# Reordered projections, halved softplus and paced clears in a Perceiver block with a selective scan

## The reference, cut to what matters

```
x = x + attention(layernorm(x), ctx)              # q, k, v of width 512, reshaped to (-1, 16, 64)
n = layernorm(x)
xi = n @ x_proj.T                                 # 1024 channels
xc = silu(causal_conv4(xi) + conv_b)
delta = softplus(n @ dt_proj.T + dt_b)
B, C = n @ B_proj.T, n @ C_proj.T                 # 16 states
h[s] = exp(delta * A[s]) * h[s] + delta * B[s] * xc    # along the 64 tokens, for each state s
y = sum over s of h[s] * C[s] + D * xc
x = x + y @ out_proj.T
x = x + experts(layernorm(x))                     # 16 experts, 4 per token, chosen by routed scores
```

## Time and profile before

| | us |
|---|---|
| three runs, median | 1340.01 |
| lowest, highest | 1334.44, 1340.54 |
| the profiled execution | 1334.18 |
| its span (first to last instruction) | 1332.2 |
| clearing: first issue of a clear | 84.94 |
| first projections of groups 0, 1, 2, 3 start on PE | 124.3, 353.1, 576.0, 798.7 |
| first block of the experts on PE | 898.98 |
| last slots of group 2 (dispatch begins) | 875.12 |

### The profile page before, as it was taken

The page is one execution under the profiler, slowest core; times in us unless marked ns, Lnnn a source line. Parts: engine busy times, 40 slices in busy tenths (PEclk is TensorE's granted clock), DMA queues, the critical chain, the costliest instruction groups (busy, mean ns, idle before and its releaser), DMA issues.

```text
span 1332.2 us, 13289 instructions
## 1 busy us (share of the span) xinstructions
PE 1143.1 (86%) x4276; PEld 729.0 (55%) x4276; DVE 881.5 (66%) x946; ACT 621.5 (47%) x1366; POOL 134.0 (10%) x113
## 2 busy tenths in 40 slices
PE   6988769789797899998889989629999999999992
PEld 4875646566564567675557757324444445444451
DVE  1311579666757999967799995877999974224312
ACT  4542665435355655537556635624455422222321
POOL 0010003201000043000007000030000000233002
PEclk9998889989998999999899999759999998999997
DMA  8375006998601145340035331068999984999994
GB/s 281 111 245 194 4 17 221 404 396 326 223 9 16 33 125 175 78 145 0 17 72 150 119 123 44 0 225 274 360 357 351 375 316 152 375 357 406 410 382 126
DMA packets 115188, 266.27 MB, mean 200 GB/s; under 512 B 11280, under 2 KB 44208, under 8 KB 115120
## 3 DMA queue, kind: packets, MB, share of 16 engines
q1 hardware_dynamic: 99248, 207.22, 45.1%
q0 software_dynamic: 15872, 58.20, 11.1%
HBM read 197.07 MB, written 68.32 MB: 199 GB/s over the span
## 4 chain that ended last, share of the span: by engine, by line
PE 46%; DVE 35%; DMA 8%; ACT 7%; issue 3%; POOL 1%; SPq 0%; POOLq 0%; DVEq 0%; ACTq 0%
DVE state L1348 12%; PE bank L815 9%; PE bank L776 7%; DVE state L1345 6%; PE bank L683 5%; PE bank L695 4%; PE bank L836 4%; PE bank L716 4%; DVE decay L1352 3%; DMA ctx<-in_ctx_t 3%; DVE state L1355 3%; DVE y_acc L1359 2%; PE bank L632 2%; DMA bc_bcast<-bc_scratch 2%; PE bank L747 2%
## 5 line engine op out<-in xcount | busy, mean ns | idle before, releaser
L1348 DVE TENSOR_TENSOR_SCAN state<-decay,state 128x2048 f32<-128x2048 f32 x64 | 282.9, 4421 | 23.5 <-ACT decay L1102 22.6
L815 PE MATMUL bank<-expert_w,block_x_t 128*128 128x512 f32 x496 | 227.0, 601 | 1.8 <-ACT block_x_t L1154 1.7
L683 PE MATMUL bank<-decay,params 128*128 128x512 f32 x384 | 173.3, 595 | 5.9 <-DVE decay L1352 5.9
L1639 POOL DMA_INDIRECT dispatched<-ffn_x,slot x32 | 73.0, 2280 | 756.3 <-DVE slot L1441 747.7
L1102 ACT ACTIVATE decay<-delta_even,params 128x256 f32<-128x256 f32 x256 | 107.2, 498 | 82.7 <-PE bank L683 74.2
L815 PEld LDWEIGHTS bank<-expert_w,block_x_t 128*128 128x128 f32 x496 | 91.6, 195 | 93.7 <-issue 91.6
L695 PE MATMUL bank<-ctx,queries_ctx 128*128 128x256 f32 x512 | 125.6, 403 | 16.2 <-DMA ctx<-in_ctx_t 15.0
L716 PE MATMUL bank<-probs,ctx 128*128 128x256 f32 x512 | 121.2, 392 | 11.1 <-ACT probs L1009 6.4
L1102 ACT ACTIVATE decay<-delta_odd,params 128x256 f32<-128x256 f32 x256 | 106.2, 499 | 34.5 <-PE bank L683 24.9
L695 PEld LDWEIGHTS bank<-ctx,queries_ctx 128*128 128x128 f32 x512 | 102.1, 204 | 34.2 <-DMA ctx<-in_ctx_t 16.4
L1496 DVE SCALAR_TENSOR_TENSOR hidden<-hidden,bank 128x256 f32<-128x256 f32 x62 | 26.1, 421 | 142.7 <-ACT hidden L1158 141.7
(11 more groups left out here) (193 smaller groups left out, 1334.2 us busy)
## 6 DMA issues: line engine op xcount, KB each, us to landing
dispatched<-ffn_x POOLq DMA_DIRECT2D x38, 1024.0 KB, 27.2
expert_w<-in_eg_t SPq DMA_DIRECT2D x62, 512.0 KB, 6.4
expert_w<-in_eu_t SPq DMA_DIRECT2D x62, 512.0 KB, 9.6
expert_w<-in_ed_t SPq DMA_DIRECT2D x62, 512.0 KB, 9.6
ctx<-in_ctx_t SPq DMA_DIRECT2D x32, 512.0 KB, 7.5
ctx<-in_ctx_n SPq DMA_DIRECT2D x32, 512.0 KB, 4.1
bc_bcast<-bc_scratch SPq DMA_DIRECT2D x64, 256.0 KB, 5.8
block_x<-dispatched SPq DMA_DIRECT2D x62, 256.0 KB, 9.0
```

Of the source, the lines that this page charges most:

```text
L683: mm = pe.matmul(y_bank[c][:, :], ident, dA[(g * NS + j) % NDEC][:, c * 512:(c + 1) * 512], start=False, stop=(j == NS - 1))
L815: mm = pe.matmul(o, xbT[q % 2][:, c, :], w_gu[q % NW][:, :, c, :], start=(c == 0), stop=(c == DC - 1))
L1348: dve.tensor_tensor_scan(h, dA[n % NDEC][:, 0:sw], h, 0.0, ALU.mult, ALU.add).then_inc(scan_rd, 1)
L1639: pool.indirect_dma_start(xd[WAVE_OF[c]], bass.IndirectOffsetOnAxis(slot[:, i:i + 1].bitcast(U32), 0), fx[:, t, :], None).then_inc(dispatc ...
```

## The change

It does six things. (1) The xp weights are loaded and multiplied before the dt weights, in SP's, PE's and ACT's lists; the scratch of softplus and tanh moves into the place of the xp weights. (2) The sums of states 14 and 15 come after all eight jobs, and `copy_sum` after the logarithm (for group 3's boundary: before it). (3) Softplus runs in two halves, the first after the second dt job, the tanh after the third; `scan_inputs` takes the tanh product first and then each half. (4) DVE puts the three parts of state 15 between the four convolutions, where before all of it stood ahead of them. (5) State 0 of group 3 is finished before the tokens of group 2 are normed, and `y_start(3)` goes ahead of that group's `norm_std`; the expert weights of blocks 1 and 2 are loaded after the first three token blocks. (6) The clears start at the same point as before, but each waits until the one before it has landed.

```
 CLEARS = [(w, r, min(r + CLEAR_ROWS, ROWS[w])) for w in range(len(WAVES)) for r in range(0, ROWS[w], CLEAR_ROWS)]
-CLEAR_UNITS = range(8, 16)
+CLEAR_FROM = 8
 JMAX = max(CAP) // P
...
 LEAD, TAIL, PRE = 4, 2, 2
-LN_AFTER = 3
 SCAN_PARTS = 4
...
                 out += [("probs", UNIT0[g] + k)]
-        out += [("v", g)] * DC + [("norm2", g)] * NTS[g] + [("bc", g)] + [("dt", g)] * (NBK // 2) + [("xp", g)] * (NBK // 2)
+        out += [("v", g)] * DC + [("norm2", g)] * NTS[g] + [("bc", g)] + [("xp", g)] * (NBK // 2) + [("dt", g)] * (NBK // 2)
         if g + 1 < NGR:
...
             xp = QT_[:, 4096:8192].rearrange("p (c n) -> p c n", c=DC)
-            sp_tmp = [QT_[:, 0:NBK * GTS[g]] for g in range(NGR)]
-            th_tmp = [QT_[:, SW:SW + NBK * GTS[g]] for g in range(NGR)]
+            sp_tmp = [QT_[:, 2 * SW:2 * SW + NBK * GTS[g]] for g in range(NGR)]
+            th_tmp = [QT_[:, 3 * SW:3 * SW + NBK * GTS[g]] for g in range(NGR)]
         del_s = [(del_0, del_1)[g % 2][:, 0:NBK * GTS[g]] for g in range(NGR)]
...
                 sp.wait_ge(x1_rdy, g + 1)
+                sp.dma_start(xp, xp_t.rearrange("(c p) n -> p c n", p=P)).then_inc(xpw_in, 16)
                 sp.dma_start(dtw, dt_t.rearrange("(c p) n -> p c n", p=P)).then_inc(dtw_in, 16)
-                sp.dma_start(xp, xp_t.rearrange("(c p) n -> p c n", p=P)).then_inc(xpw_in, 16)
             def bc_of(g):
...
                 if w == 0:
-                    for j in range(NW):
+                    load_gate_up(w, 0)
+                    load_down(w, 0)
+                    for j in range(NX):
+                        load_block_x(w, j)
+                    for j in range(1, NW):
                         load_gate_up(w, j)
                         load_down(w, j)
-                    for j in range(NX):
-                        load_block_x(w, j)
                     load_bc((NGR - 1) * NS + 3)
...
                 mm.then_inc(a_full, 1)
-                for w, landed in ((dtw, dtw_in), (xp, xpw_in)):
+                for w, landed in ((xp, xpw_in), (dtw, dtw_in)):
                     pe.wait_ge(landed, 16 * (g + 1))
...
                         mm.then_inc(a_full, 1)
-                        if g > 0 and w is dtw and k == NBK - 2:
-                            sum_state(g - 1, NS - 2)
-                        if g > 0 and w is xp and k == 2:
-                            sum_state(g - 1, NS - 1)
+
+                if g > 0:
+                    for s in range(NS - PRE, NS):
+                        sum_state(g - 1, s)
             def out_proj(g):
...
                 ins.then_inc(a_free, 1)
-            def softplus_exp(g):
-                act.wait_ge(a_free, CONV_JOBS[g])
-
-                step(act.activation(sp_tmp[g], del_s[g], ACT.Abs))
-                act.activation(sp_tmp[g], sp_tmp[g], ACT.Exp, scale=-1.0).then_inc(act_step, 1)
+            def halves(v, g, half):
+
+                n = NBK * GTS[g] // 2
+                return v[g][:, half * n:(half + 1) * n]
+
+            def softplus_exp(g, half):
+
+                act.wait_ge(a_free, ja.n)
+                v = halves(sp_tmp, g, half)
+                step(act.activation(v, halves(del_s, g, half), ACT.Abs))
+                act.activation(v, v, ACT.Exp, scale=-1.0).then_inc(act_step, 1)
                 chain.n += 1
...
                 act.wait_ge(act_step, chain.n)
-                act.activation(sp_tmp[g], sp_tmp[g], ACT.Ln, bias=1.0).then_inc(sp_rdy, 1)
+                for half in range(2):
+                    v = halves(sp_tmp, g, half)
+                    act.activation(v, v, ACT.Ln, bias=1.0).then_inc(sp_rdy, 1)
             def silu(g):
...
                 for k in range(0, NBK, 2):
-                    proj_dt(g, k)
+                    proj_x(g, k)
                     if late:
...
                 for k in range(0, NBK, 2):
-                    proj_x(g, k)
-                    if k == 0:
-                        softplus_exp(g)
-                    if k == 2 * (LN_AFTER - 1):
-                        softplus_ln(g)
-                    if g > 0 and k == 2:
-                        copy_sum(g - 1)
-                silu(g)
+                    proj_dt(g, k)
+                    if k == 4:
+                        silu(g)
+                    if k % 4 == 2:
+                        softplus_exp(g, k // 4)
+                if g == NGR - 1:
+                    copy_sum(g - 1)
+                softplus_ln(g)
+                if 0 < g < NGR - 1:
+                    copy_sum(g - 1)
                 if g + 1 < NGR:
...
             scan_decay(NGR - 1, 0)
+            y_start(NGR - 1)
             norm_std(NTS[NGR - 2])
             ffn_copy(NGR - 2)
-            y_start(NGR - 1)
             ffn_logits(NGR - 2)
...
                 d = del_s[g]
-                dve.wait_ge(sp_rdy, g + 1)
-                step(dve.scalar_tensor_tensor(out=d, in0=d, scalar=0.0, in1=sp_tmp[g], op0=ALU.max, op1=ALU.add))
                 dve.wait_ge(tanh_rdy, g + 1)
-
                 step(dve.scalar_tensor_tensor(out=th_tmp[g], in0=th_tmp[g], scalar=1.0, in1=u_s[g],
                                               op0=ALU.add, op1=ALU.mult))
-                step(dve.scalar_tensor_tensor(out=u_s[g], in0=th_tmp[g], scalar=0.5, in1=d,
-                                              op0=ALU.mult, op1=ALU.mult))
+                n = NBK * GTS[g] // 2
+                for half in range(2):
+                    h = slice(half * n, (half + 1) * n)
+                    dve.wait_ge(sp_rdy, 2 * g + half + 1)
+                    step(dve.scalar_tensor_tensor(out=d[:, h], in0=d[:, h], scalar=0.0, in1=sp_tmp[g][:, h],
+                                                  op0=ALU.max, op1=ALU.add))
+                    ins = dve.scalar_tensor_tensor(out=u_s[g][:, h], in0=th_tmp[g][:, h], scalar=0.5, in1=d[:, h],
+                                                   op0=ALU.mult, op1=ALU.mult)
+                step(ins)
                 first = d.rearrange("p (m t) -> p m t", t=T)[:, :, 0:1]
...
                     norm_apply(TILE0[g + 2], NTS[g + 2], NT, mv1_, rstd1, TILE0[g + 2])
-                for s in range(PRE):
+                for s in range(PRE - 1):
                     scan_step(g, late.pop(0))
                 for k in range(0, NBK, 2):
+                    if k // 2 in range(SCAN_PARTS - 1):
+                        scan_step(g, late[0], parts=(k // 2,))
                     conv(g + 1, k)
                 scan_inputs(g + 1)
-                if g + 1 < NGR - 1:
-                    scan_step(g + 1, 0, parts=(0, 1, 2))
+                scan_step(g + 1, 0)
                 add_tiles(g)
                 ffn_norm(g)
-                if g + 1 < NGR - 1:
-                    scan_step(g + 1, 0, parts=(3,))
-            scan_step(NGR - 1, 0, parts=(0, 1))
             route(NGR - 2)
-            scan_step(NGR - 1, 0, parts=(2, 3))
             slots(NGR - 2)
...
             pool.wait_ge(zero_rdy, 1)
+            pool.wait_ge(s_full, CLEAR_FROM)
             for i, (w, first, end) in enumerate(CLEARS):
-                n = CLEAR_UNITS[i * len(CLEAR_UNITS) // len(CLEARS)]
-                pool.wait_ge(s_full, n)
+                if i:
+                    pool.wait_ge(cleared, 16 * i)
                 v = xd[w][first:end].rearrange("(p r) d -> p r d", p=P)
...
```

## The result

The changed kernel took 1290.4 us (median of 4 runs, 1288.5 to 1291.31), the kernel before 1340.28 beside it (1334.44 to 1341.49): a ratio of 0.966, 95% interval 0.9618 to 0.9702. The forecast was 1295, its range 1281 to 1316. The profiled span fell from 1332.2 to 1289.4, by 42.8 us; the sum forecast 41.1.

| point | before | after | gained so far | by this stage | forecast |
|---|---|---|---|---|---|
| first projection, group 0 | 124.31 | 119.34 | 5.0 | 5.0 | 4.5 |
| first decay, group 0 | 165.83 | 159.73 | 6.1 | 1.1 | 3.5 |
| issue of the weights, group 1 | 342.17 | 309.43 | 32.7 | 26.6 | 25.8 |
| first projection, group 1 | 353.13 | 323.73 | 29.4 | -3.3 | 0.7 |
| first projection, group 2 | 576.02 | 538.44 | 37.6 | 8.2 | 5.3 |

A forecast was written before the change was run, and what follows sets the result against it. Bound: a chain of unlike stages, group 1's attention on transfers beside clears, group boundaries on a chain over all engines. Terms 5 - 0.5 + 26.5 + 3.5 + 10.6 - 2.5 - 1.5 = 41.1 us gave 1293.1, forecast 1295, range 1281 to 1316.

The forecast's parts named there:

- Attention 0: Up to group 0's first projection: last `ctx_n` lands sooner with one clear in flight, 5 us, less 0.5 for xp weights.
- What bounds attention 1: Group 1's attention waits on transfers slowed by queued clears, not arithmetic; pacing wins 25.8 us up to the weights' issue.
- The weights of group 1: From issue of group 1's projection weights to its first projection: they land sooner with paced clears, 0.7 us gained.
- Group 0: From group 0's first projection to its first decay, with no sums or state between: 3.5 us gained (0 to 6).
- Boundaries 1 and 2: At the boundaries of groups 1 and 2 queries resume 5.3 us earlier each, set by `out_proj` and no longer DVE.
- The last boundary: Group 3's first projection to group 2's last slots: state 0 now precedes the routing, slots about 6 us later.
- The handover: From the slots to the first expert block: last dispatch lands within 4 us instead of 7.43, 3.5 us gained.
- the weights: Expert weights of blocks 1 and 2, now after the first token blocks: 1.5 us lost (0 to -7.5).
- The end: The last stretch, from group 3's `out_proj` to the kernel's end: no gain forecast, 0 us.
- Clears still slow attention 1: Rival: one clear in flight is almost always moving, `ctx_t` stays late, half of 26.5 us lost: 1308 us; 17%.
- clears late: Rival: 40 landings in a row end late and hold DVE at `ffn_norm(0)`; at 9 us a clear, 1363 us; 5%.
- boundaries give nothing: Rival: convolutions hold ACT, ACT holds PE, late sums hold `out_proj`; 10.6 us and half of 3.5 lost: 1307; 13%.

The follow-up runs named there:

- the first run: The kernel before with only the paced clears, each clear waiting for the one before it: 1302.36 us, 0.9786 of the kernel before.
- the second run: The changed kernel without the paced clears, back in bursts of five at units 8 to 15: 1324.07 us, 0.9944 of the kernel before.

## Why the prediction was right, point by point

- **Attention 0** (4.5, measured 5.0): right. PE waited 0.74 us for the last probabilities in place of 4.62 for a `ctx_n`, and the 16 matmuls behind it took 3.72 us in place of 5.27.
- **What bounds attention 1** (25.8, measured 26.6): right, both sides were run. The paced clears alone took 28.6 us off the way to group 1's weights, and without them all of it was gone. DVE waited 2.7 us for broadcasts, in the kernel before 31.3. The pace was mis-sized, though: the forecast took DVE's 10.17 us a state, 50.8 for five, and 3 us of loss to transfers over eight units; from 214.78 to 267.92 five states took 53.1 us. The excess is two waits of 1.19 us for a broadcast, but PE ran 10.78 us a unit without a pause meanwhile, so they did not set the time. What was left of the loss in attention 1 was PE's work, not a transfer. That the gain comes of the pacing, and not of the clears' earlier place, the run with late clears shows (23.5 of 26.6 us). The reason given, that the gap between clears is what helps, is only partly shown: with hardly a gap (q0 and q1 fill 96.7% of the engines' time), two clears in the queue and only three units of overlap, attention 1 lost 1.7 us, where the kernel before, by the forecast's count, lost 28.8 over eight units with five to ten clears in the queue.
- **The weights of group 1** (+0.7, measured -3.3): the step that failed is the end of the clears, 317 us forecast, 347 measured. A clear took 6.6 us and not 5.8 (alone it needs 4.82, less than the 5.3 that the forecast read, but sharing costs far more than the half a us allowed), so the last ones lay on the xp weights (14.26 us to land). The forecast's own times did not fit each other here: its gains put the issue of these weights at 342.2 - 33.8 = 308.4 us, ahead of clears that end at 317, and yet it let them land sooner than before. The run with earlier clears shows the cause: 10.26 us.
- **Group 0** (3.5, measured 1.1): the list is that of the forecast from the second job on, jobs 3.46 us apart. But the first ACT copy came 5.6 us after PE's start, not 3.95, 1.7 of the 2.4 us. The table of busy time has the granted clock of the first 6 us (third figure from the end), changed kernel and kernel before:

```profile
119.30:125.30 6.00, 5.96 (x19) 4.98 (x20) 0.00 (x0) 0.33 (x1) 0.71 (x1) 0.68 1.03 418
```
```profile
124.30:130.30 6.00, 6.00 (x28) 5.33 (x28) 0.00 (x0) 1.21 (x3) 0.00 (x0) 0.96 0.45 176
```

  Why it was lower was not tried. The other 0.7 us are not traced.
- **Boundaries 1 and 2** (5.3 each, measured 8.2 and 8.8): the mechanism was right in the steps that set the time, `out_proj` at 38.4, delta 7.3 us earlier (forecast 8.4), the bound moved from DVE to `out_proj`. Mis-sized was the term behind it. I compared the restart of the queries only; the pause before the restart also had a price, 16 matmuls in 6.70 us instead of half of 7.33. 6.70 - 3.67 = 3.0 us, which with 5.3 makes 8.3.
- **The last boundary** (-6, measured -8.5): 3.8 us are state 0, as the run with the old order shows. The term missed is `out_proj`'s start: I compared delta (45.0, measured 45.8) and took the later sums and `copy_sum` as free, as for the groups before; there `out_proj` had started at 38.0, here at 34.6, and it went to 38.4. That is 3.8 of the other 4.7 us.
- **The handover** (3.5, measured 2.5) and **the weights** (-1.5, measured -1.8): right. The last dispatch landed in 3.83 us instead of 7.43.
- **The end** (0, measured 4.2): not in the sum. The last stretch ran without the two drops of the clock that the kernel before had in its middle; what decides when the clock drops there stays open.
- **The rivals.** "Clears still slow attention 1" fell by the first run, "clears late" by the 34 us of slack (the forecast had 58), "boundaries give nothing" by the two boundaries and by the second run (0.9944, interval below 1). It was near, though: without the pieces of state 15, or with the sums in between, each boundary loses 6 to 8.7 us.

The errors were +0.5, -2.4, +0.8, -4.0, +2.9, +3.5, -2.5, -1.0, -0.3 and +4.2 us, in the order of the table; the total of 1.7 is smaller than most of them, and partly luck. The median came out 4.6 us below the 1295 forecast; 1.9 of them are what the forecast had added to its sum, 1293.1.

## What to carry to other kernels

When two queues share the DMA engines, count their packets: here a bulk transfer in packets of 3.85 KB took three quarters of the bandwidth (258 of 338 GB/s) from loads in packets of 1.20 KB as long as it was queued. Keep its queue short, and place it so that it ends before the next load that somebody waits for. A late barrier cost its full length here: know the slack before slowing what it waits for.

When a list is reordered, write out all engines and follow the buffers of the copies, since the bank that ACT has not freed stops PE two jobs later. A pause of several us removed from PE was worth more than its length here, as the work behind it also ran faster.

## What the runs showed of the hardware

- A clear of 1 MB alone goes out every 4.82 us; beside two weight loads, 13.2 us.
- After pauses of 6 to 7 us PE ran the next work slower: 16.70 us for 32 matmuls of 512 columns after 6.78 us (14.00 after 1.28), 16.70 for 64 of 256 columns after 6.21 us (14.1 in a row). The granted clock of the first 7 us was 0.61 and 0.62, and 1.00 in the changed kernel's `out_proj`.
- POOL's indirect dispatches took 0.95 to 1.02 us each to issue while DVE was doing small work, and 3.04, 4.10 and 2.08 us once DVE had begun a state at 844.02 (in the kernel before 1.94, 4.08 and 2.09, with a state begun at 880.73); POOL's timeline of the changed kernel:

```profile
841.51 0.96 POOL L1652 DMA_INDIRECT dispatched<-ffn_x,slot  x1 [0.30 <-issue]
...
844.10 3.04 POOL L1652 DMA_INDIRECT dispatched<-ffn_x,slot  x1 [0.30 <-issue]
847.44 4.10 POOL L1652 DMA_INDIRECT dispatched<-ffn_x,slot  x1 [0.30 <-issue]
```

That the state is the cause was not tried.
